# Cross-attention of a decoder: scores in four row groups, softmax on whole tiles, counts by additions, constants and statistics prepared in self-attention

## The reference

```python
def _L1_xattn_ref(q, k, v, Wq, bq, Wk, bk, Wv, bv, Wo, bo):
    ...
    qh = (q @ Wq.T + bq).reshape(B, Nq, H, D).transpose(0, 2, 1, 3)      # H = D = 16
    kh = (k @ Wk.T + bk).reshape(B, Nkv, H, D).transpose(0, 2, 1, 3)
    vh = (v @ Wv.T + bv).reshape(B, Nkv, H, D).transpose(0, 2, 1, 3)
    attn = jax.nn.softmax(jnp.einsum('bhqd,bhkd->bhqk', qh, kh) * scale, axis=-1)
    out = jnp.einsum('bhqk,bhkd->bhqd', attn, vh)
    out = out.transpose(0, 2, 1, 3).reshape(B, Nq, C)
    return out @ Wo.T + bo
...
x = x + _L1_attn_ref(_layernorm(x, axis=-1), L1_attn_wq, L1_attn_wk, L1_attn_wv, L1_attn_wo)
x = x + _L1_xattn_ref(_layernorm(x, axis=-1), ctx_1024, ctx_1024, L1_xattn_Wq, L1_xattn_bq, ...)
x = x + _L1_ffn_ref(_layernorm(x, axis=-1), L1_ffn_wg, L1_ffn_bg, L1_ffn_Wgate, ...)
```

## Time and profile before

| what | us |
|---|---|
| runs | 3345.52, 3356.22, 3368.39; median 3356.22 |
| profiled execution | 3359.07, its span 3357.5 |
| PE busy | 2944.8 (88%) |
| DVE busy | 2063.2 (61%) |
| GpSimd busy | 1508.6 (45%) |
| ACT busy | 1418.0 (42%) |

### The profile page before, as it was taken

The page is one execution under the profiler, slowest core; times in us unless marked ns, Lnnn a source line. Parts: engine busy times, 40 slices in busy tenths (PEclk is TensorE's granted clock), DMA queues, the critical chain, the costliest instruction groups (busy, mean ns, idle before and its releaser), DMA issues. The chain is left out here.

```text
span 3357.5 us, 43453 instructions
## 1 busy us (share of the span) xinstructions
PE 2944.8 (88%) x15258; PEld 1880.4 (56%) x15258; DVE 2063.2 (61%) x3889; ACT 1418.0 (42%) x2701; POOL 1508.6 (45%) x1189
## 2 busy tenths in 40 slices
PE   5998898899877679589999999979996999999998
PEld 2343343343334565355555555546665888888887
DVE  4999999998996545366666666638874222222221
ACT  5667757667652202145555455435551111111111
POOL 4797887888774440133333333227763111111111
PEclk8999999999998689599999999989996999999999
DMA  7135235225410261012222222220113656656562
GB/s 222 45 108 152 70 84 152 94 59 152 129 24 12 85 221 44 16 37 59 48 48 48 55 54 48 46 87 8 48 50 130 209 180 198 191 186 201 176 205 66
DMA packets 279944, 339.83 MB, mean 101 GB/s; under 512 B 84228, under 2 KB 236992, under 8 KB 279728
## 3 DMA queue, kind: packets, MB, share of 16 engines
q1 hardware_dynamic: 256479, 303.54, 30.4%
q0 software_dynamic: 16704, 27.21, 3.4%
q10 hardware_dynamic: 6544, 6.30, 0.6%
HBM read 231.55 MB, written 104.80 MB: 100 GB/s over the span
## 5 line engine op out<-in xcount | busy, mean ns | idle before, releaser
L489 POOL TENSOR_TENSOR mb_drive<-mb_dtx,mb_b_rep 128x1024 f32<-128x1024 f32 x256 | 598.9, 2356 | 178.0 <-DVE mb_pD L412 77.1
L791 PE MATMUL mb_pY<-mb_hc,ident 128*128 128x512 f32 x1024 | 503.0, 616 | 63.0 <-DVE mb_hc L423 62.6
L1763 DVE TENSOR_REDUCE at_nm_of<-at_pS 128x1 f32<-128x512 f32 (+3 forms) x768 | 408.1, 554 | 227.9 <-PE at_pS L1755 114.7
L1828 ACT ACTIVATE at_e<-at_pE 128x512 f32<-128x512 f32 x576 | 326.4, 598 | 355.3 <-PE at_pE L1819 353.4
L1835 POOL TENSOR_SCALAR_AFFINE_SELECT at_e<-at_e 128x256 f32<-128x256 f32 x256 | 156.4, 629 | 599.6 <-ACT at_e L1828 598.3
L2913 POOL DMA_INDIRECT out<-et_y,et_to x71 | 112.0, 1577 | 660.1 <-DVE et_y L2967 407.0
L2957 DVE TENSOR_TENSOR et_mT<-et_silu,et_pU 128x512 f32<-128x512 f32 (+1 forms) x160 | 100.3, 627 | 469.9 <-ACT et_silu L2928 469.9
L791 PEld LDWEIGHTS mb_pY<-mb_hc,ident 128*128 128x128 f32 x1024 | 189.9, 195 | 336.6 <-issue 179.1
L1751 PE MATMUL at_pS<-at_kT,at_qT 64*128 64x512 f32 (+3 forms) x768 | 304.5, 448 | 72.0 <-DVE at_nm_of L1763 67.3
L2928 ACT ACTIVATE et_silu<-et_pG 128x512 f32<-128x512 f32 (+1 forms) x160 | 87.8, 549 | 651.6 <-PE et_pU L2989 651.6
L537 ACT ACTIVATE mb_pD<-mb_dt,mb_a_neg 128x512 f32<-128x512 f32 x384 | 259.6, 688 | 154.6 <-DVE mb_hc L423 143.5
(11 more groups left out here) (456 smaller groups left out, 5039.3 us busy)
## 6 DMA issues: line engine op xcount, KB each, us to landing
t_wg<-in_t_wgT SPq DMA_DIRECT2D x40, 1024.0 KB, 6.3
t_wu<-in_t_wuT SPq DMA_DIRECT2D x40, 1024.0 KB, 9.0
t_wd<-in_t_wdT SPq DMA_DIRECT2D x40, 1024.0 KB, 11.4
mb_b_rep<-mb_rows SPq DMA_DIRECT2D x64, 512.0 KB, 6.1
mb_c_rep<-mb_rows SPq DMA_DIRECT2D x64, 512.0 KB
t_h_sorted<-blank SPq DMA_DIRECT2D x6, 4160.0 KB, 21.9
t_h_sorted<-blank SPq DMA_DIRECT2D x18, 1170.0 KB, 6.7
t_h_sorted<-blank SPq DMA_DIRECT2D x12, 1040.0 KB, 6.1
```

The lines of the kernel that those rows point to most:

```text
L489: nc.gpsimd.tensor_tensor(drive[G % RINGS][:, :, :], dtx[:, m, :].unsqueeze(1).to_broadcast([P, 2, CH]), b_rep[:, 2 * j:2 * j + 2, :], ALU ...
L791: last = nc.tensor.matmul(pY[:, :], K.ident[:, :], hc[G % RINGS][:, k, :], start=False, stop=(j == PAIRS - 1 and k == 1))
L1763: nc.vector.tensor_reduce(nm_of[:, w0 // 512, a, qb:qb + 1], pS[a][:, 0:w1 - w0], axis=AX.X, op=ALU.max, negate=True).then_inc(s_max, 1)
L1828: nc.scalar.activation(e[g % NE][:, a, :], pE[a][:, :], ACT.Exp).then_inc(s_ex, 1)
```

## The change

Scores: the keys are masked for two heads (`ktwo`), and one matmul contracts 32 rows and gives 2 x 77 = 154 columns; eight matmuls in four row groups, each group with its own PSUM bank of one tile `pS`, make the scores of all 16 heads. They are one group in PE's list, behind T3. Largest, subtraction and sums are one DVE instruction each for a whole tile; ACT still takes two exponentials, both waiting for the whole subtraction. The order of the heads in `e` changes with it, and both halves of weighing take something from all four transposed groups, so half 0 waits for the copy of T3.

Counts: the sum of `pairs` over the tiles of a chunk is made by four dependent additions (`count`), placed between the small steps of `shares`; `sofar` holds the count before each tile, and `places` has two matmuls.

Self-attention: DVE takes bn_stats of each finished tile at the end of its list and bn_aggr at the start of the tile after; SP loads context, weights and biases of cross-attention behind its other transfers of tiles 8, 11, 14, 17 and 20.

Setup: the block itself loads only `bv` and `bo`. DVE adds epsilon for all tiles first, GpSimd takes the power of chunk 0, DVE normalises chunk 0, GpSimd chunk 1. PE's order is keys, transposes, queries, scores of tile 0, values. `kT` lies in the third `e` buffer. In the loop the layer-norm statistics of coming chunks are gone from DVE, and a power per chunk from GpSimd.

```diff
@@ _attend
+        def dve_stats(eng, t):
+            eng.wait_ge(s_res, t + 1)
+            if t >= 2:
+                eng.wait_ge(s_moments, t - 1)
+            nc.vector.bn_stats(stats[:, t % 2, :], row_of(R, t)).then_inc(s_bn, 1)
+        def dve_moments(eng, t):
+            eng.wait_ge(s_bn, t + 1)
+            nc.vector.bn_aggr(K.cross.moments[:, t, :], stats[:, t % 2, :]).then_inc(s_moments, 1)
...
+            if i >= 2:
+                dve_moments(eng, i - 2)
             scores(0, 0, 3)
...
             scores(8, 0, 2)
+            if before:
+                dve_stats(eng, i - 1)
...
                 sync(eng, i, i, **flags(i))
+                if 8 <= i < 8 + 3 * CrossConstants.PARTS and i % 3 == 2:
+                    K.cross.load(eng, (i - 8) // 3, s_cross)
...
+            dve_moments(eng, NT - 2)
+            dve_stats(eng, NT - 1)
+            dve_moments(eng, NT - 1)
@@ class CrossConstants, load: two transfers to a part
+        if part == 0:
+            for k in range(KD):
+                start(self.ctxT[:, k, :, :], io["ctxT"][:, k * P:(k + 1) * P, :].rearrange("b p s -> p b s"))
+        elif part == 1:
+            matrix(self.wk, "xa_wkT")
+            matrix(self.wv, "xa_wvT")
...
@@ _cross_attention, vector
-                nc.vector.tensor_reduce(top[m][:, :].rearrange("p (g x) -> p g x", g=2), scores(m), axis=AX.X, op=ALU.max).then_inc(s_top, 1)
+                nc.vector.tensor_reduce(of_group(top), scores, axis=AX.X, op=ALU.max).then_inc(s_top, 1)
...
+            def count(ch, t):
+                now, then = sofar[ch % 2], sofar[(ch + 1) % 2]
+                if ch + t > 0:
+                    eng.wait_ge(s_sofar, ch * TC + t)
+                if t == TC - 1 and ch > 0:
+                    eng.wait_ge(s_A, NTH["PL0", ch - 1] + 1)
+                out = now[:, t + 1, :] if t < TC - 1 else then[:, 0, :]
+                nc.vector.tensor_tensor(out, now[:, t, :], pairs[:, t, :], ALU.add).then_inc(s_sofar, 1)
...
-                for lag, half in ((-8, (0, 1)), (-7, (2, 3))):
-                    ch = chunk_at(n, lag, 2)
-                    if ch is not None:
-                        statistics(0, ch, half)
-                ch = chunk_at(n, -6, 2)
-                if ch is not None:
-                    moments(0, ch)
-                    variance(0, ch)
@@ scalar
-                eng.wait_ge(s_sub, 2 * n + m + 1)
+                eng.wait_ge(s_sub, n + 1)
@@ tensor
+                for m in range(KD):
+                    for r in range(4):
+                        part = slice(32 * r, 32 * r + 32)
+                        last = nc.tensor.matmul(pS[:, r, m * 2 * CTX:(m + 1) * 2 * CTX], qT[n // TC % 2][part, m, t * P:(t + 1) * P],
+                                                ktwo[part, m, b, :, :].rearrange("p a s -> p (a s)"), start=True, stop=True,
+                                                skip_group_check=True)
...
-                eng.wait_ge(s_read, NTH[f"T{2 * m + 1}", n] + 1)
+                if m == 0:
+                    eng.wait_ge(s_read, NTH["T3", n] + 1)
...
-                for t in range(1, TC):
-                    last = nc.tensor.matmul(part(t, TC), ones[:, :], pairs[:, 0:TC - t, :].rearrange("p t e -> p (t e)"), start=False, stop=(t == TC - 1))
+                last = nc.tensor.matmul(out[:, 0:TC * NE], ones[:, :], sofar[ch % 2][:, :, :].rearrange("p t e -> p (t e)"), start=False, stop=True)
...
             for n in range(DRAIN):
-                for g in range(2):
+                for g in range(4):
                     if 2 <= n < NT + 2:
                         turns(n - 2, g)
                 if n + 1 < NT:
-                    scores(n + 1, 0)
-                for g in range(2, 4):
-                    if 2 <= n < NT + 2:
-                        turns(n - 2, g)
-                if n + 1 < NT:
-                    scores(n + 1, 1)
+                    scores(n + 1)
```

More of the change, by code:

```diff
@@ L2181, in _, with __init__, load, start @@
             pe_final(eng, NT - 1)
+class CrossConstants:
+    PARTS = 5
+    def __init__(self, K, ctx):
+        sb = lambda n, shape: K.sb(ctx, f"xc_{n}", shape)
+        NE = K.io["t2_router"].shape[1]
+        self.moments = sb("moments", [P, NT, 2])
+        self.ctxT = sb("ctxT", [P, KD, NB, CTX])
+        self.wq, self.wk, self.wv, self.wo = (sb(n, [P, KD, D]) for n in ("wq", "wk", "wv", "wo"))
+        self.bq, self.bk = sb("bq", [P, KD]), sb("bk", [P, KD])
+        self.router, self.router_b = sb("router", [P, KD, NE]), sb("router_b", [P, NE])
+        self.nc, self.io, self.loads = K.nc, K.io, 0
+    def load(self, eng, part, s_cross):
+        io = self.io
+        def start(dst, src):
+            self.loads += 1
+            eng.dma_start(dst, src).then_inc(s_cross, 16)
+        def matrix(dst, name):
+            start(dst[:, :, :], io[name].rearrange("(k p) n -> p k n", p=P))
+        if part == 0:
[4 more added lines that the diff above has]
+            matrix(self.wv, "xa_wvT")
+        elif part == 2:
+            matrix(self.wq, "xa_wqT")
+            matrix(self.wo, "xa_woT")
+        elif part == 3:
+            matrix(self.router, "t2_router")
+            start(self.router_b[:, :], io["t2_router_b"].partition_broadcast(P))
+        else:
+            with self.nc.allow_non_contiguous_dma(reason="256 biases, one to a partition"):
+                start(self.bq[:, :], io["xa_bq"].rearrange("(k p) -> p k", p=P))
+                start(self.bk[:, :], io["xa_bk"].rearrange("(k p) -> p k", p=P))
 def fill_rows(K, eng, sorted_, part, parts, s_fill):
@@ L2278, in _cross_attention @@
         row_f = sb("row_f", [P, len(SLOTS)])
[L2279 removed]
+        pS = K.ps(c, "xa_pS", [P, 4, 512])
         pT = [K.ps(c, f"xa_pT{q}", [P, CH]) for q in range(2)]
@@ L2706, in turn, with scores @@
                 return bank(name, ch)
-            def scores(n, m):
+            def scores(n):
                 b, t = n // (TC * CPB), n % TC
-                if t == 0 and m == 0:
+                if t == 0:
                     eng.wait_ge(s_read, NTH["Q1", n // TC] + 1)
                 if n > 0:
-                    eng.wait_ge(s_sub, 2 * n - 1 + m)
-                for r in range(2):
-                    part = slice(64 * r, 64 * r + 64)
-                    last = nc.tensor.matmul(pS[m][:, r, 0:4 * CTX], qT[n // TC % 2][part, m, t * P:(t + 1) * P],
-                                            kfour[part, m, b, :, :].rearrange("p a s -> p (a s)"), start=True, stop=True)
+                    eng.wait_ge(s_sub, n)
+                for m in range(KD):
+                    for r in range(4):
[3 more added lines that the diff above has]
+                                                skip_group_check=True)
                 last.then_inc(s_S, 1)
@@ L2791, in _ @@
                 transposes("LN", 0, k)
+            for m in range(KD):
+                queries(0, m)
+            eng.wait_ge(s_kp, 2 * KD)
+            scores(0)
             for b in range(NB):
@@ L2838, in _ @@
             out = turn("CN0", 0)
-            eng.wait_ge(s_sofar, NCH)
-            nc.tensor.matmul(out[:, 0:NE], ones[:, :], sofar[NCH % 2][:, :], start=True, stop=True).then_inc(s_A, 1)
+            eng.wait_ge(s_sofar, NCH * TC)
+            nc.tensor.matmul(out[:, 0:NE], ones[:, :], sofar[NCH % 2][:, 0, :], start=True, stop=True).then_inc(s_A, 1)
 def _expert_slots(K, table, weights, s_w, load_weights):
```

234 lines of the change are left out of this document (104 added, 130 removed).

## The result

The changed kernel took 3327.13 us (median of 5 runs, 3320.16 to 3328.14), the kernel before 3358.09 (5 runs beside them, 3345.52 to 3368.39): a ratio of 0.9904, 95% interval 0.9877 to 0.9932. The forecast was 3330.

The account below looks back on a forecast made before the run. PE was taken as busiest (88%) and the loop's bound, a load as the setup's. Terms -10.2, 0, -7.4, -6.3 and -2.5 sum to -26.4: 3359.07 profiled gives 3332.7, less 2.9 for the median, 3330; range 3312 to 3347.

Parts of the forecast that it names:

- Setup, -10.2: Cross-attention's setup: load wait gone, queries ahead of values, first transposes of weights 10.2 us earlier; bounds -8.8 and -12.2.
- Statistics and loads, 0: Self-attention: bn_stats and bn_aggr (0.54) fit into DVE's idle 1.20 at tile borders; the loads also cost 0.
- Scores, 0.72: Each tile's scores on PE: four row groups run together, 0.72 us for the whole tile, 1.44 before.
- Rivals C: Each tile's scores: only two row groups at a time, 1.26 us; +3.3 for -7.4, total 3340; chance 0.1.
- D: Each tile's scores: row groups of 32 don't overlap, 2.35 us; total 3373, or 3464 with loads exposed; chance 0.05.
- The order of a tile, -7.4: Loop tiles: weighing waits for ACT's copies; 16 ordinary tiles gain 0.09 us each, 14 with filled gaps 0.43.
- Places, -6.3: Routing places: three fewer matmuls save 4.0 us over six loop chunks; the tail saves 1.28 twice, less 2 x 0.15.
- DVE, -2.5: Loop: PE's 2.5 us of waits for DVE's subtraction go; its 7.0 for the residual additions aren't shortened.
- the loop is bound by PE: Cross-attention's loop over tiles: in an ordinary tile of 5.41 us PE's groups follow each other with nothing between.
- Rival A: DVE's places: count additions meet GpSimd's long instructions, so residual additions and product come late; 12.6 us, total 3342; chance 0.2.
- product waits more than 7 in all: Sign in the loop that Rival A holds: PE's product waits more than 7 us in total.
- Rival B: Loop chunks: with less DVE work, long chunks fall to the shortest; 12 us more gain, total 3318; chance 0.2.

Follow-up runs that it names:

- first pair: First profiled executions of the changed kernel and of the kernel before; spans 3326.4 and 3357.5 us.
- second pair: One more profiled execution each of the changed kernel and the kernel before, both unedited; spans 3333.2 and 3360.5 us.
- e8: Changed kernel with its ten loads of weights, context and biases issued at cross-attention's start, not during self-attention; 3349.86 us, 0.9977 of the kernel before.
- e12: Changed kernel with each tile's bn_stats and bn_aggr in self-attention done three times; 3340.99 us, 0.9927 of the kernel before.
- e11: Changed kernel with places as before: counts by one reduction and one addition, five matmuls; 3340.14 us, 0.9951 of the kernel before.
- e9: Changed kernel with DVE's logits work behind the next tile's subtraction and ACT's small exponential ahead of T0 and T1 copies; 3319.34 us, 0.9896 of the kernel before.
- e5: The kernel before, run once more unedited; one run, 3362.01 us.
- e1: The changed kernel, run again unedited; 3344.25 us, 0.9924 of the kernel before.
- e6: Changed kernel with DVE's work on the logits moved behind the next tile's subtraction; 3336.57 us, 0.9928 of the kernel before.
- e10: As e9, with the next chunk's normalised rows made by ACT instead of GpSimd; 3323.96 us, 0.9917 of the kernel before.
- e3: Changed kernel with DVE's addition to the residual moved right behind the subtraction, ahead of places; 3346.19 us, 0.9916 of the kernel before.
- e7: Changed kernel with logits behind the next subtraction, residual addition ahead of places, both exponentials behind all four copies; 3344.84 us, 0.9950 of the kernel before.

## Why the prediction was right, and where only its sum was

- **Setup, -10.2.** Right: -10.0 in the first pair, -11.5 in the second. First scores 11.0 behind the start, and 13.0 from there to T0 where 12.7 was taken. e8 shows the loads to be 9.3 of it.
- **Statistics and loads, 0.** Right (e12 for the statistics, e8 for the loads, and PE's waits for the maxima in self-attention are 67.8 against 67.3).
- **Scores, 0.72.** Right: 0.74. Rivals C (1.26) and D (2.35) are refuted, all four groups of 32 rows run together.
- **The order of a tile, -7.4.** The walk was right in kind: weighing waits for ACT's copy, T2 starts at 1.27. In an ordinary tile T3's copy ended 3.27 behind T0, as worked out, but weighing started 0.15 behind it and not 0.07, at 3.42 and not 3.34, and the 0.09 a tile melted. Where other work fills the gap, PE is through the scores at 3.09 and not 3.00 (T2 and T3 take 1.08 to the scores, not 1.01), so the tile gains 0.34 and not 0.43; in the chunks with scatters it is waited away. Measured, with DVE's part, 2.5 in eight tiles and 4.4 to 7.1 in five chunks.
- **Places, -6.3.** Wrong in the loop, where nothing of 4.0 came (e11). In the tail 1.9 to 2.9 came for 2.3, which is luck in part: the two places that the term counts gave 0.6 together, as the additions cost 0.64 and 0.71 and not 0.15 each.
- **DVE, -2.5.** PE's waits for the subtraction went (2.5 and 3.2 before, 0.6 and 0.9 after). That the waits for the residual aren't shortened was right: 7.0 and 8.1 before, 9.9 and 6.7 after.

The step that failed is "the loop is bound by PE". It is so in the 12 tiles without scatters. In the ordinary ones of these, waits for ACT's copies add 0.50 a tile. In the chunks behind, the chain from logits over DVE, the small exponential, DVE's places and residual addition to PE's product sets the pace, and a microsecond off PE ahead of that product comes back as a wait, there or elsewhere. -13.9 was forecast for the loop; the first pair gives -9.6, the second -7.0. e9 cuts that chain and gets 15.3.

That the total agreed with the medians so well is probably luck: scatter stood on the right side. The three steady stages give -19.6 (second pair -18.5). To them comes a tail of -2 (76.0 against 77.6, both with the stall) to -5 (67.9 in e8, whose tail is the changed kernel's, against 72.6 in e5 beside it): -21 to -25 together. The interval of the first comparison is -23 to -41 us, that of e1 -16 to -35. The granted clock differs where the gain is large: in e1 it was 0.945 in the mean of the runs against 0.941 of the kernel before, and -25 us; in e6, whose five chunks take the same 167.5 as the changed kernel's, 0.942 against 0.940, and -22. Whether the change has a part in that clock is open, but self-attention at 838.3 to 840.0 in e6 to e8, beside 838.5 in e5, doesn't point to it.

Rival A (0.2) had named this place. Its criterion "product waits more than 7 in all" tells nothing apart, as the kernel before has 7.0 and 8.1 and the changed one 9.9 and 6.7; its mechanism was there, mostly in neighbours of the additions. Of the 32 additions of counts the median took 0.166 and the longest 2.31, but the logits' bias and the instruction behind the small exponential lasted 2.40 and 2.02 beside GpSimd. By the Trainium skill ("SBUF — State Buffer", who interferes with whom) VectorE and GpSimd share a port pair, which the first to start holds for its whole instruction while the other blocks. The trace agrees in kind: both ended within 0.06 us of GpSimd's instruction. But the kernel before has such long instructions too (1.84 and 2.10), the price of 12.6 didn't come, and e11, without the three further additions, has the same five chunks. Rival B (chunks under 31) happened only in e9 and e10; its own "against", that ACT's small exponential comes no earlier, is what e9 removed.

What stays open: the stalls of 5 us in the tail, in some executions of both kernels, for which the traces give no cause; and whether e9 beats the changed kernel by its full 15 us, as the two were not run side by side. Against e11, the changed kernel with places undone, it is 20.8 us faster, with a granted clock of 0.946 against 0.942.

## What to carry to other kernels

Look for a loop's bound in each kind of its iterations, and where one engine waits 2 to 3 us at the same point of every round, follow that wait back across engines before counting savings on any of them: here PE was the busiest and yet late by DVE's order. Removing one link only moved the wait (e3, e6), and so did three moves that left the small exponential late (e7); the gain came with logits and small exponential moved together (e9). So a null result of one move doesn't acquit the chain or prove the next suspect. And stages that the change doesn't touch belong in the comparison: they differed by 12 us here, as much as the largest part of the change.

## What the runs showed of the hardware

- Four row groups of 32 ran together: 16 passes of 154 columns in 0.74, against 1.24 for eight passes of 308 in two groups of 64. In four groups each streams 616 columns, in two 1232; at the 0.89 ns of the earlier trace rows that is 0.55 and 1.10, an estimate that leaves 0.19 and 0.14 for going over from one kind of matmul to the other.
- TensorE's granted clock fell from 1.0 to 0.5 during an idle time of 2.59 us in the loop and stayed there for 6.8 us, and the product behind the idle time took 2.05 instead of 1.13. With the wait gone (e9) it stayed full in two of three chunks.
- An addition of DVE with both inputs in SBUF, 32 columns wide, started 0.05 behind the first of two back-to-back instructions of GpSimd (1.22 each) and ended 0.06 behind the second: it lasted 2.40, and was not let in between the two. The same stands in e9, 2.38.
- A power on GpSimd took 1.02 us for 4 columns and 4.80 for 28 (setup of the changed kernel); the second stood ahead of the rows of chunk 1.
- Self-attention's stretch came at 822.9 (twice) to 840.0 over fourteen profiled executions, longer with each hundredth less of granted clock (0.97, 0.96, 0.95), with the statistics of either kernel and with e12's: 17 us of scatter from this stage alone.
